# Final loads that wait for the counted blocks, a table load moved ahead of the expert blocks, and the closing additions split between two engines

## The chip, the cores and the metric

The kernel runs on one core of a Trainium2 chip. The core has five engines that run their own instruction streams and meet at semaphores: TensorE (PE) multiplies matrices into PSUM banks, VectorE (DVE) and ScalarE (ACT) read and write PSUM and SBUF, GpSimd (POOL) works on SBUF alone and issues the indirect transfers, SyncE (SP) issues most other transfers. The metric is the device time of one execution in microseconds (us); lower is better.

## The reference

A gated block on x (8 batches of 128 tokens, width 128): cross attention with 16 heads, then a mixture of 8 experts, of which each token takes 2, beside a shared expert.

```python
x = x + tanh(g_xattn) * attention(layernorm(x), ctx, ctx, mask)
n = layernorm(x)
shared = (silu(n @ shared_gate.T) * (n @ shared_up.T)) @ shared_down.T
probs = sigmoid(n @ router_w.T + routing_bias)
scores, indices = top_k(probs, 2);  scores /= scores.sum(-1)
w = zeros(tokens, 8);  w[token, indices] += scores
combined = sum over e of w[:, e] * ((silu(n @ gate_w[e]) * (n @ up_w[e])) @ down_w[e])
x = x + tanh(g_ffn) * (shared + combined)
```

The inputs are drawn from a fixed seed. Counted from the reference on them, the eight experts get 393, 406, 155, 274, 99, 207, 206 and 308 of the 2,048 choices.

## The kernel before

Everything is ordered by hand: each engine's stream is written out, with waits on named semaphores.

**Attention** takes the first 115 us or so. While its last groups run, the tokens are **routed**: batches are taken in five parts (`ROUTED`, the last, `LAST`, is batch 7). For each part PE transposes the normalised rows (`x2_transposes`) into a PSUM bank of `route_bank`, ACT copies them (`x2_split`), PE computes the router's logits, ACT takes an exponential (`route_exp`, whose last call is the last exponential of the program), DVE chooses the two experts (`choose_steps`), PE counts (`ranks`), DVE turns ranks into places (`place`), and POOL scatters the rows to a table `xs` in HBM (`scatter`), sorted by expert and cut into candidate tiles of 128 rows. `table_steps` lists which tiles exist, for full tiles of the first six batches first (`EARLY` = 5 blocks), then for the rest.

**Blocks.** The number of tiles in use depends on the data. The program always runs `BLOCKS` = 23 of them, the most that there can be; the blocks past the last existing tile read an empty tile whose row numbers point outside the result. Each block n is gathered by SP (`gather`, 8 buffers), transposed by PE (`block_transpose`), split by ACT and DVE into a high and a low part (`block_hi`, `block_lo`), multiplied with gate and up weights (`block_gate_up`), put through SiLU on ACT (`block_silu`) and a product on DVE (`block_hidden`), transposed again, copied by DVE (`block_hidT`), multiplied with the down weights (`block_down`), scaled by ACT (`block_y`), and scattered by POOL into `ys` in HBM, which counts `y_out[n % 8]` up by 16 when it has landed. PE works on several blocks at once in a software pipeline.

**The shared expert** has four units (`shared_pass(unit, part)`, `silu(unit)`, `hidden(unit)`): two of 128 hidden columns for each half of the tokens, each of six matmuls over 512 tokens; then `down_step(half)` and `add_shared(half)`, which adds a half of the tokens into `x_sb` on DVE (`acc_done`). Unit 0 runs among the blocks, units 1 to 3 after them.

**The end.** SP waits until all y scatters have landed (`y_out`), issues four loads `load_y` of 256 KB from `ys` into `y_rows` (`in_y`), DVE adds each token's two expert results to `x_sb` in four pieces, two additions each (`first_added`, `sum_ready`), and after each piece SP or ACT stores it. `stay_warm(n)` is n matmuls on a constant tile whose results nobody reads.

## Time and profile before

| | us |
|---|---|
| median of 3 runs (lowest, highest) | 181.72 (181.02, 184.23) |
| the profiled execution, whole time | 181.07 |
| its span, from the first to the last instruction | 179.3 |
| PE busy in it | 165.0 |
| DVE, ACT, POOL busy in it | 126.9, 109.3, 108.4 |
| mean granted clock of PE, 1 being full speed | 0.993 |

The profile is one execution; its rows give times from the start of the span. The whole time is 1.8 us longer than the span. An engine's busy time says how much of the span it worked, not that the end waited for it.

### The profile page before, as it was taken

What the parts mean: (1) busy time and instruction counts of PE and PEld (TensorE: products, weight loads), DVE (VectorE), ACT (ScalarE), POOL (GpSimd) and SP (SyncE); (2) the same over time, 40 slices, a digit from 0 to 9 for tenths busy, and PEclk for the clock granted to TensorE, in tenths of its full rate; (3) what the DMA queues carried; (4) which work ended last, traced back from release to release, by engine and by line L of the source; (5) the groups of instructions that cost most, each with busy time, mean ns of one, the idle gap of its engine ahead of it and who ended that gap; (6) DMA issues with size and microseconds to landing.
All of it is one profiled execution on the core that took longest, in us unless ns stands there. A gap on an engine that the chain in (4) does not pass through costs nothing.

```text
span 179.3 us, 4668 instructions
## 1 busy us (share of the span) xinstructions
PE 165.0 (92%) x1424; PEld 140.2 (78%) x1424; DVE 126.9 (71%) x613; ACT 109.3 (61%) x402; POOL 108.4 (60%) x137
## 2 busy tenths in 40 slices
PE   7899889999999999999999999988899999998960
PEld 7777669988889998779998779876586887886840
DVE  2779988756898766798776798778746666663364
ACT  3657997468588267598367698513546666663210
POOL 3666799846796816866706868686444666666200
PEclk9999999999999999999999999999999999999997
DMA  5999994900000000101000000013132222211063
GB/s 154 262 372 375 412 410 191 385 23 4 16 0 18 0 2 4 32 19 44 1 4 0 15 21 32 15 49 91 45 89 65 63 66 78 73 53 35 12 223 117
DMA packets 11095, 17.34 MB, mean 97 GB/s; under 512 B 2075, under 2 KB 6945, under 8 KB 10944
## 3 DMA queue, kind: packets, MB, share of 16 engines
q1 hardware_dynamic: 9504, 14.59, 24.0%
q0 software_dynamic: 1280, 2.20, 3.7%
q8 instruction: 12, 0.20, 0.4%
q10 hardware_dynamic: 288, 0.26, 0.4%
q14 instruction: 11, 0.09, 0.2%
HBM read 9.99 MB, written 7.51 MB: 98 GB/s over the span
## 4 chain that ended last, share of the span: by engine, by line
PE 62%; DVE 13%; ACT 8%; DMA 6%; POOL 5%; issue 4%; SPq 1%
PE misc L397 8%; PE pt L650 7%; PE s_even L360 6%; PE o_bank L386 6%; ACT probs L716 4%; PE pt L371 4%; PE proj_q L317 3%; DMA wq_raw<-wqT 3%; PE proj_k L317 3%; DVE probs L925 3%; PE proj_k L319 2%; PE pt L641 2%; PE proj_k L318 2%; PE proj_q L319 2%; PE proj_q L318 2%
## 5 line engine op out<-in xcount | busy, mean ns | idle before, releaser
L716 ACT ACTIVATE probs<-probs,negmax 128x128 f32<-128x128 f32 x128 | 50.0, 395 | 8.5 <-DVE negmax L925 8.5
L1311 POOL TENSOR_TENSOR probs<-probs,rinv 128x512 f32<-128x512 f32 x32 | 33.1, 1046 | 24.6 <-DVE rinv L939 24.3
L1420 POOL DMA_INDIRECT ys<-probsT,xg x23 | 22.5, 979 | 17.2 <-issue 10.7
L716 ACT ACTIVATION_READ_ACCUMULATOR probs<-probs,negmax 128x1 f32 x128 | 24.4, 191 | 0.0
L925 DVE CUSTOM_DVE_ANT_0 probs<-s_even,mask 128x128 f32<-128x128 f32 x64 | 18.1, 282 | 3.8 <-issue 3.8
L1341 POOL DMA_INDIRECT xs<-xrow,slot x16 | 16.3, 1019 | 6.5 <-issue 3.9
L371 PE MATMUL pt<-ident_sb,probs 128*128 128x128 f32 x128 | 17.6, 277 | 1.6 <-POOL probs L1311 1.1
L360 PE MATMUL s_odd<-kT,qT 64*128 64x128 f32 x128 | 18.5, 285 | 0.0
L360 PE MATMUL s_even<-kT,qT 64*128 64x128 f32 x128 | 18.5, 284 | 0.0
L925 DVE CUSTOM_DVE_ANT_0 probs<-s_odd,mask 128x128 f32<-128x128 f32 x64 | 18.1, 283 | 0.0
L650 PEld LDWEIGHTS pt<-down_sb,v 128*128 128x128 f32 x92 | 12.1, 190 | 7.2 <-issue 7.1
L705 ACT COPY qT<-proj_q 128x512 f32<-128x512 f32 x12 | 7.1, 588 | 16.7 <-PE proj_q L319 16.7
L360 PEld LDWEIGHTS s_even<-kT,qT 64*128 64x128 f32 x128 | 15.4, 188 | 2.1 <-issue 1.4
L371 PEld LDWEIGHTS pt<-ident_sb,probs 128*128 128x128 f32 x128 | 14.1, 141 | 3.4 <-issue 1.8
L650 PE MATMUL pt<-down_sb,v 128*128 x92 | 15.7, 293 | 1.2 <-DVE v L1237 1.2
L386 PE MATMUL o_bank<-probsT,v 128*64 128x128 f32 x240 | 16.4, 279 | 0.0
L386 PEld LDWEIGHTS o_bank<-probsT,v 128*64 128x64 f32 x240 | 12.8, 137 | 3.4 <-issue 2.5
L360 PEld LDWEIGHTS s_odd<-kT,qT 64*128 64x128 f32 x128 | 15.4, 188 | 0.0
L397 PE MATMUL misc<-wo_sb,oT 128*128 128x128 f32 x112 | 14.3, 281 | 0.9 <-DVE oT L947 0.9
L397 PEld LDWEIGHTS misc<-wo_sb,oT 128*128 128x128 f32 x112 | 13.0, 192 | 2.0 <-DVE oT L947 1.7
L912 DVE COPY kT<-proj_k 128x512 f32<-128x512 f32 x12 | 8.3, 692 | 5.7 <-PE proj_k L319 5.6
L852 ACT ACTIVATE probsT<-pt,xg 128x128 f32<-128x128 f32 x23 | 8.4, 367 | 6.2 <-PE pt L650 4.3
(279 smaller groups left out, 455.0 us busy)
## 6 DMA issues: line engine op xcount, KB each, us to landing
xs<-pad SPq DMA_DIRECT2D x5, 858.0 KB, 5.8
xg<-xs SPq DMA_DIRECT2D x23, 66.0 KB, 1.9
down_sb<-down SPq DMA_DIRECT2D x1, 1152.0 KB, 8.9
probs<-ys SPq DMA_DIRECT2D x4, 256.0 KB, 4.0
gu_raw<-gu SPq DMA_DIRECT2D x3, 256.0 KB, 6.5
wk_raw<-wkT SPq DMA_DIRECT2D x2, 256.0 KB, 3.8
wq_raw<-wqT SPq DMA_DIRECT2D x2, 256.0 KB, 5.0
mask<-mask SPq DMA_DIRECT2D x8, 64.0 KB, 2.0
```

What stands on the lines that cost most here:

```text
L317: pe.matmul(dst, a_hi, b_hi, start=True, stop=False)
L360: mm = pe.matmul(s_bank[odd][:, j * P:(j + 1) * P], qT[rows, 4 * half + j, i * P:(i + 1) * P], kT[rows, 4 * half + j, i * P:(i + 1) * P], ...
L371: mm = pe.transpose(pt_bank[u][:, j * P:(j + 1) * P], probs[:, r, 4 * u + j, :], ident_sb[:])
L386: mm = pe.matmul(o_of.get(g, o_bank)[DK * odd:DK * (odd + 1), j * P:(j + 1) * P], v_sb[i][:, h * DK:(h + 1) * DK], probsT[:, half, 2 * j + ...
L397: mm = pe.matmul(misc[:, 0:P], oT[:, c // 4, c % 4, :], wo_sb[:, c, :], start=(c == 0), stop=(c == CHUNKS - 1))
L650: mm = pe.matmul(y_bank[:, 0:P], hidT[n % 2][:, c, :], down_sb[:, bass.ds(e * I_FFN + c * P, P)], start=(c == 0), stop=(c == 1))
L716: e = act.activation(probs[:, r, l, :], probs[:, r, l, :], ACT.Exp, bias=negmax[:, r, l:l + 1], scale=-1.0, accum_out=rowsum[:, r, l:l + 1])
L852: act.activation(y_sb[n % IN_FLIGHT][:], y_bank[:, 0:P], ACT.Copy, scale=xg[n % IN_FLIGHT][:, P + 1:P + 2]).then_inc(y_ready, 1)
L925: dve.tensor_tensor_reduce(probs[:, r, l, :], s_bank[l % 2][:, (l // 2) * P:(l // 2 + 1) * P], mask_sb[r // 2][:], -1.0, HUGE, ALU.add, AL ...
L1311: pool.tensor_tensor(quad, quad, rinv[:, r, 4 * u:4 * u + 4].unsqueeze(2).to_broadcast([P, 4, P]), ALU.mult).then_inc(norm_done, 1)
L1341: pool.indirect_dma_start(out=xs, out_offset=bass.IndirectOffsetOnAxis(ap=slot[:, b, k:k + 1], axis=0), in_=xrow[:, b, k, :], in_offset=No ...
L1420: pool.indirect_dma_start(out=ys, out_offset=bass.IndirectOffsetOnAxis(ap=xg[n % IN_FLIGHT][:, P:P + 1].bitcast(U32), axis=0), in_=y_sb[n ...
```

## The change

Seven edits, all after the attention.

1. DVE computes, from the number of late tiles, how many scatters each of the eight `y_out` semaphores has counted once all **existing** blocks have landed (`quota_steps`, two small instructions after block 11's product). SP reads these eight numbers into registers and waits by them before `load_y`. It waits for all 23 scatters only at the very end, after the stores.
2. The first addition of each piece goes to POOL, directly after the loads land and with no wait for the shared expert. DVE makes the second addition of two pieces, then `add_shared` of that half, which now comes last; the stores wait for `acc_done`.
3. ACT takes a SiLU of one column (`act_scratch`) directly behind the last routing exponential. The compiler then puts SiLU's table load there instead of ahead of block 0's SiLU.
4. Shared unit 0 takes the place of `stay_warm(6)` ahead of the last routing part; unit 1 takes the place in the block loop that unit 0 had; units 2 and 3 run at the end, and both `down_step`s come after them. ACT's and DVE's parts move along: `silu(0)` and `hidden(0)` into blocks 0 and 1.
5. `ranks(LAST)` stands ahead of `block_transpose(1)`.
6. The last two routing parts use the banks `pt0` and `pt1`, which the attention leaves free, and the shared units and down steps other banks.
7. `x2_transposes` of these parts wait for those banks alone.

```diff
+FEWEST = TOKENS * TOP_K // P // IN_FLIGHT
...
-        shared_banks = [(proj_bank["q"], proj_bank["k"]), (o_bank, misc), (s_bank[0], s_bank[1]), (proj_bank["q"], proj_bank["k"])]
-        d_bank = [pt_bank[0], proj_bank["q"]]
+        shared_banks = [(proj_bank["q"], proj_bank["k"]), (proj_bank["q"], proj_bank["k"]), (o_bank, misc), (s_bank[0], s_bank[1])]
+        d_bank = [proj_bank["k"], proj_bank["q"]]
-        route_bank = [misc, misc, proj_bank["q"], proj_bank["q"], proj_bank["k"]]
+        route_bank = [misc, misc, proj_bank["q"], pt_bank[0], pt_bank[1]]
...
         def store_out(engine, n):
             tiles = slice(2 * n, 2 * n + 2)
-            engine.wait_ge(sum_ready, n + 1)
+            engine.wait_ge(acc_done, 1 + n // 2)
...
+            def quota(i):
+                return sp.value_load(quotas[0:1, i:i + 1], min_val=16 * FEWEST, max_val=16 * (FEWEST + 1))
+
+            sp.wait_ge(quota_ready, 2)
+            due = [quota(i) for i in range(IN_FLIGHT)]
             for i in range(IN_FLIGHT):
-                sp.wait_ge(y_out[i], 16 * len(range(i, BLOCKS, IN_FLIGHT)))
+                sp.wait_ge(y_out[i], due[i])
             for n in range(4):
                 load_y(sp, n)
             store_out(sp, 0)
             store_out(sp, 2)
+            for i in range(IN_FLIGHT):
+                sp.wait_ge(y_out[i], 16 * len(range(i, BLOCKS, IN_FLIGHT)))
             sp.wait_ge(out_sem, 64)
...
                 if r == LAST:
-                    pe.wait_ge(k_free, PROJ_USES * PAIRS)
+                    pe.wait_ge(pt1_free, GROUPS)
+                elif r == 3:
+                    pe.wait_ge(pt0_free, GROUPS)
                 elif r:
                     pe.wait_ge(at_ready, r)
-                if r == 3:
-                    pe.wait_ge(counts_read, 1)
...
-            stay_warm(6)
+            pe.wait_ge(counts_read, 1)
+            shared_pass(0, 0)
+            shared_pass(0, 1)
             x2_transposes(LAST)
...
             block_transpose(0)
-            block_transpose(1)
             pe.wait_ge(in_down, 16)
             pe.wait_ge(ez_ready, LAST + 1)
             ranks(LAST)
+            block_transpose(1)
             block_gate_up(0, experts[0])
             for n in range(BLOCKS):
                 if n + 2 == EARLY:
-                    pe.wait_ge(counts_read, 2)
-                    shared_pass(0, 0)
-                    shared_pass(0, 1)
+                    pe.wait_ge(h_done, 1)
+                    shared_pass(1, 0)
+                    shared_pass(1, 1)
...
             pe.wait_ge(xglo_ready, BLOCKS)
-            shared_pass(1, 0)
+            shared_pass(2, 0)
             block_down(BLOCKS - 1, experts[BLOCKS - 1])
-            shared_pass(1, 1)
-            pe.wait_ge(h_done, 1)
-            shared_pass(2, 0)
             shared_pass(2, 1)
-            down_step(0)
+            pe.wait_ge(hid_ready, BLOCKS)
             shared_pass(3, 0)
             shared_pass(3, 1)
+            down_step(0)
             down_step(1)
...
             route_exp(LAST)
+            act.activation(act_scratch[:], warm[:, 0:1], ACT.Silu)
...
+                if n == 0:
+                    silu(0)
                 if n + 2 == EARLY:
-                    silu(0)
+                    silu(1)
             block_y(BLOCKS - 1)
-            for unit in range(1, 4):
+            for unit in range(2, 4):
                 silu(unit)
...
+            def quota_steps():
+
+                beyond = float(IN_FLIGHT * FEWEST - EARLY) + 0.5
+                dve.tensor_scalar(more[:], iota_sb, beyond, upto[:, CANDIDATES - 1:], ALU.add, ALU.is_le).then_inc(quota_ready, 1)
+                dve.wait_ge(quota_ready, 1)
+                dve.tensor_scalar(quotas[:], more[:], 16.0, 16.0 * FEWEST, ALU.mult, ALU.add).then_inc(quota_ready, 1)
...
+                if n == 1:
+                    hidden(0)
...
                 if n + 1 == EARLY:
-                    hidden(0)
+                    hidden(1)
+                if n == 2 * EARLY:
+                    quota_steps()
             block_hidT(BLOCKS - 1)
-            for unit in range(1, 4):
+            for unit in range(2, 4):
                 hidden(unit)
-            add_shared(0)
-            y_of = y_rows.rearrange("p (b k) h -> p b k h", k=TOP_K)
-            for n in range(4):
-                tiles = slice(2 * n, 2 * n + 2)
-                if n == 2:
-                    add_shared(1)
-                dve.wait_ge(acc_done, 1 + n // 2)
-                dve.wait_ge(in_y[n], 16)
-                dve.tensor_tensor(x_sb[:, tiles, :], y_of[:, tiles, 0, :], x_sb[:, tiles, :], ALU.add).then_inc(first_added, 1)
-                dve.wait_ge(first_added, n + 1)
-                dve.tensor_tensor(x_sb[:, tiles, :], y_of[:, tiles, 1, :], x_sb[:, tiles, :], ALU.add).then_inc(sum_ready, 1)
+            for half in range(2):
+                for n in (2 * half, 2 * half + 1):
+                    tiles = slice(2 * n, 2 * n + 2)
+                    dve.wait_ge(first_added, n + 1)
+                    dve.tensor_tensor(x_sb[:, tiles, :], y_of[:, tiles, 1, :], x_sb[:, tiles, :], ALU.add).then_inc(second_added, 1)
+                dve.wait_ge(second_added, 2 * half + 2)
+                add_shared(half)
...
+            for n in range(4):
+                tiles = slice(2 * n, 2 * n + 2)
+                pool.wait_ge(in_y[n], 16)
+                pool.tensor_tensor(x_sb[:, tiles, :], y_of[:, tiles, 0, :], x_sb[:, tiles, :], ALU.add).then_inc(first_added, 1)
```

What this does to the order of instructions, at three places. The names of a row are the result and what it is made from; `kT` holds block products and SiLU results here, `qT` the shared products, `pt` the two banks pt0 and pt1, `probs` the loaded expert results.

ACT at the start of the blocks, before, from the last routing exponential (`ez`) to block 1's SiLU:

```order
L747 ACTIVATE ez<-s_odd 128x8 [waits hot_ready,lg_done]
L840 CAST xg_hi<-o_bank 128x128 [waits tx_done]
L840 CAST xg_hi<-misc 128x128 [waits tx_done]
L846 ACT_TABLE_LOAD
L846 ACTIVATE kT<-s_even 128x256 [waits bg_done]
L840 CAST xg_hi<-o_bank 128x128 [waits bg_done,tx_done]
L846 ACTIVATE kT<-s_odd 128x256 [waits bg_done]
```

The same stretch of ACT in the changed kernel:

```order
L758 ACTIVATE ez<-s_odd 128x8 [waits hot_ready,lg_done]
L846 ACT_TABLE_LOAD
L846 ACTIVATE act_scratch<-warm 128x1
L852 CAST xg_hi<-o_bank 128x128 [waits tx_done]
L852 CAST xg_hi<-misc 128x128 [waits tx_done]
L858 ACTIVATE kT<-s_even 128x256 [waits bg_done]
L852 CAST xg_hi<-o_bank 128x128 [waits bg_done,tx_done]
L858 ACTIVATE kT<-s_odd 128x256 [waits bg_done]
L831 ACTIVATE kT<-proj_q 128x512 [waits gu_done]
```

The table load moved ahead of the splits of blocks 0 and 1, with one small instruction behind it, and the shared unit's SiLU of 512 columns came in behind block 1's.

DVE at the end of the program, before, from the last two shared products:

```order
L1182 TENSOR_TENSOR qT<-kT,s_odd 128x512 [waits silu_done]
L1182 TENSOR_TENSOR qT<-kT,proj_k 128x512 [waits silu_done]
L1188 SCALAR_TENSOR_TENSOR x_sb<-pt,tanh_g,x_sb 128x512 [waits d_done]
L1271 TENSOR_TENSOR x_sb<-probs,x_sb 128x256 [waits in_y0,acc_done]
L1273 TENSOR_TENSOR x_sb<-probs,x_sb 128x256 [waits first_added]
L1271 TENSOR_TENSOR x_sb<-probs,x_sb 128x256 [waits in_y1,acc_done]
L1273 TENSOR_TENSOR x_sb<-probs,x_sb 128x256 [waits first_added]
L1188 SCALAR_TENSOR_TENSOR x_sb<-proj_q,tanh_g,x_sb 128x512 [waits d_done]
...
```

The same end of DVE in the changed kernel:

```order
L1203 TENSOR_TENSOR qT<-kT,misc 128x512 [waits silu_done]
L1203 TENSOR_TENSOR qT<-kT,s_odd 128x512 [waits silu_done]
L1292 TENSOR_TENSOR x_sb<-probs,x_sb 128x256 [waits first_added] x2
L1209 SCALAR_TENSOR_TENSOR x_sb<-proj_k,tanh_g,x_sb 128x512 [waits d_done,second_added]
L1292 TENSOR_TENSOR x_sb<-probs,x_sb 128x256 [waits first_added] x2
L1209 SCALAR_TENSOR_TENSOR x_sb<-proj_q,tanh_g,x_sb 128x512 [waits d_done,second_added]
```

Eight additions of 128x256 on DVE have become four, one shared product is gone from here, and the additions of the shared expert's halves close each half instead of opening it.

POOL at the end of the changed kernel (before, its last instruction is the last of the 23 scatters):

```order
L1441 DMA ys<-probsT,xg 2048x128 [waits y_ready] x23
L1447 TENSOR_TENSOR x_sb<-probs,x_sb 128x256 [waits in_y0]
L1447 TENSOR_TENSOR x_sb<-probs,x_sb 128x256 [waits in_y1]
L1447 TENSOR_TENSOR x_sb<-probs,x_sb 128x256 [waits in_y2]
L1447 TENSOR_TENSOR x_sb<-probs,x_sb 128x256 [waits in_y3]
```

The four additions stand behind all 23 scatters, and each waits for its own load.

## Rows read from the trace of the kernel before

**Rows 1.** Chain of waits, its end: start us, us, engine, result, line.

```profile
173.07 0.43 DVE x_sb L1271
173.87 0.43 DVE x_sb L1271
174.67 0.76 DVE x_sb L1188
176.70 0.42 DVE x_sb L1273
```

**Rows 2.** PE in order of time, after the blocks: start us, us, line, operation, idle before.

```profile
163.91 0.48 PE L317 MATMUL o_bank<-xn2T_hi,gu_hi 128*128 128x512 f32 x1
...
167.57 2.05 PE L571 MATMUL pt<-down_sb,qT 128*128 128x128 f32 x16
...
172.43 2.05 PE L571 MATMUL proj_q<-down_sb,qT 128*128 128x128 f32 x16 [1.41 <-DVE qT L1182]
```

**Rows 3.** POOL in order of time, scatters of blocks 20 and 22.

```profile
163.59 0.98 POOL L1420 DMA_INDIRECT ys<-probsT,xg  x1 [0.56 <-issue]
...
166.64 0.98 POOL L1420 DMA_INDIRECT ys<-probsT,xg  x1 [0.55 <-issue]
```

**Rows 4.** SP's waits: line, releaser, us in total, times, longest.

```profile
SPq L305 <- DMA ys<-probsT,xg: 11.6, 3, 8.6
```

**Rows 5.** DMA queue of the scatters from 165.9 to 168.85 us: packets, MB.

```profile
q0 software_dynamic: 64, 0.00, 1.6%
```

**Rows 6.** SP's loads of the results and ACT's last stores, by time.

```profile
168.91 1.75 SPq L219 DMA_DIRECT2D probs<-ys  x4
...
174.78 2.71 ACTq L224 DMA_DIRECT2D out<-x_sb  x2
```

**Rows 7.** Line L219, the loads: us from issue to landing.

```profile
DMA to landing us min/median/max: 3.6/4.0/4.2
```

**Rows 8.** Groups of POOL by form: count, busy us, mean ns, idle before.

```profile
L1286 POOL TENSOR_TENSOR ck_lo<-ctx_sb,ck_hi 128x256 fp32r<-128x256 f32 x3 | 2.2, 729 | 0.2
```

**Rows 9.** POOL, then DVE, in order of time, near 9 us.

```profile
8.83 1.30 POOL L1304 TENSOR_TENSOR wk_lo<-wk_raw,wk_hi 128x512 fp32r<-128x512 f32 x1 [1.65 <-ACT wk_hi L696]
...
6.99 0.73 DVE L901 TENSOR_TENSOR wq_lo<-wq_raw,wq_hi 128x512 fp32r<-128x512 f32 x1 [0.38 <-ACT wq_hi L696]
...
9.49 1.19 DVE L901 TENSOR_TENSOR wq_lo<-wq_raw,wq_hi 128x512 fp32r<-128x512 f32 x1 [0.69 <-ACT wq_hi L696]
```

**Rows 10.** ACT in order of time, at the start of the blocks.

```profile
122.47 0.18 ACT L747 ACTIVATE ez<-s_odd 128x8 f32<-128x8 f32 x1 [0.64 <-PE s_odd L437]
123.80 0.27 ACT L840 CAST xg_hi<-o_bank 128x128 fp32r<-128x128 f32 x1 [1.15 <-PE o_bank L625]
...
124.93 1.28 ACT L846 ACT_TABLE_LOAD   x1
126.22 0.38 ACT L846 ACTIVATE kT<-s_even 128x256 f32<-128x256 f32 x1
```

**Rows 11.** DVE in order of time, at the start of the blocks.

```profile
125.56 0.22 DVE L1053 TENSOR_TENSOR exists<-exists,early 128x64 f32<-128x64 f32 x1
125.82 0.29 DVE L1065 TENSOR_TENSOR_SCAN upto<-exists,none 128x64 f32<-128x64 f32 x1
126.64 0.42 DVE L1231 TENSOR_TENSOR kT<-kT,s_even 128x256 f32<-128x256 f32 x1 [0.53 <-ACT kT L846]
```

**Rows 12.** SP's gathers of blocks 5 and 6, line L289's landing, PE's transpose of block 5.

```profile
129.47 0.86 SPq L289 DMA_DIRECT2D xg<-xs  x2
...
DMA to landing us min/median/max: 1.8/1.9/2.2
...
132.44 0.27 PE L625 MATMUL misc<-ident_sb,xg 128*128 128x128 f32 x1
```

**Rows 13.** PE in order of time, the six `stay_warm` matmuls, in two passes each.

```profile
119.40 1.58 PE L584 MATMUL s_even<-warm 128*128 128x128 f32 x12 [0.45 <-issue]
```

**Rows 14.** Line L284, SP's loads of table entries into registers: ns min/median/max.

```profile
L284 SPq TENSOR_LOAD <-table x23: 267/273/457, 118.0 to 155.6; - x23
```

5 lines of the change are left out of this document (4 added, 1 removed).

## The prediction

> **What bounds the kernel now.** I read the chain of waits from its end first. From 173.07 us on it is DVE alone [rows 1]: additions of loaded results one behind the other, the second half's `add_shared` at 174.67, more additions, and the last ends at 177.12 (176.70 + 0.42). ACT's last store is issued at about 177.15 (174.78 + 2.71, less its own 0.34) [rows 6], and the span ends at 179.3: 2.2 us lie between the last DVE result and the end. Then PE in order of time [rows 2]: it leaves the blocks at 163.9, does shared units 1 to 3, stands idle for 1.41 us before the last down step and ends at 174.48 (172.43 + 2.05). Then the transfers that feed DVE: SP waits for y scatters, in one stretch for 8.6 us [rows 4], issues the four loads from 168.91 to 170.66 [rows 6], and they land 3.6 to 4.2 us after issue [rows 7], the first at 172.5. So three strands meet at 172.5 to 174.7: the loads, PE's shared expert, and DVE's own queue. Taking one away alone would give little; this change touches all three. The blocks before them run at PE's pace, 1.53 us each, and nothing in the edits makes that pace faster, so only their start can shift them.
>
> **Part 1, the loads' wait.** The counts in the reference give 4+4+2+3+1+2+2+3 = 21 tiles of 128, so blocks 21 and 22 are empty. The trace agrees: in the 2.95 us after 165.9, in which their scatters ran, the queue carried 64 packets of 0.00 MB [rows 5]. By the formula, semaphores 0 to 4 are due 48 and the others 32, which is what blocks 0 to 20 bring. POOL issued block 20's scatter at 163.59 and block 22's at 166.64 [rows 3]. The one long wait of 8.6 us began when the last gather was issued, at 157.1, so it ended at 165.7: the landing of block 20. The loads can go then instead of at 168.9, **3.1 us sooner** (3.05 by the two scatter issues). SP must read eight numbers first: 8 x 0.27 us [rows 14], 3.7 us by the slowest such row, from 157.1 on; that lies inside the 8.6 us and costs nothing. If that cover were gone it would cost 2 to 4 us. Eight waits by register instead of by constant: I take 0.05 us in all, between 0 and 0.3.
>
> **Part 2, PE at the end.** After 163.9 it now has four half units and block 22's down product, then both down steps. From 163.9 to the first down step before (167.57) were exactly four half units and that product, with a short wait for `h_done` in it; so the first down step again starts near 167.4. The two take 1.8 us each (2.05 less the overlap of 0.2), and silu(3) and hidden(3) are done under the first. PE's last result comes near **171.1 instead of 174.5**. The 1.4 us of unit 1 went to the block loop, where unit 0's were, and unit 0 went to where `stay_warm(6)` spent 1.58 us [rows 13]: six matmuls of 512 columns, which take about 1.4 us in the blocks' tail too. PE waits for the last rows there anyway, so this exchange is worth 0 (bounds -0.1 and +0.2).
>
> **Part 3, the additions.** Before, DVE had eight additions and two `add_shared` after its last product. Now POOL does four. DVE's price for a first and a second addition is 0.80 us a pair (173.87 - 173.07), of which the second is about 0.46, because it waits for the first; `add_shared` is 0.76 [rows 1]. POOL's 128x256 operation on two SBUF inputs takes 0.73 us [rows 8]; it also rounds, so a plain addition may take 0.6. I take 0.7.
>
> First without any interference, before a shift of the blocks: loads issued at 165.85, landing at 169.45, 170.2, 170.9 and 171.3 (the spread of rows 6 and 7). POOL, free since 167.6, ends its additions at 170.15, 170.9, 171.6 and 172.3. DVE takes the second piece's addition at 170.95, `add_shared(0)` from 171.4 to 172.15, the last two additions until 172.95, `add_shared(1)` until 173.7.
>
> But the two engines then work on SBUF operands at the same time, and the trace shows what that does. At 8.83 POOL began a subtraction of 1.30 us; DVE's subtraction with two SBUF inputs issued at 9.49 took 1.19 us, while the same operation at 6.99, with POOL idle, took 0.73 [rows 9]. It ended as if it had begun when POOL's ended. The Trainium skill says the same (SBUF — State Buffer, "SBUF: two separate sides"): VectorE with two SBUF inputs and GpSimd take an exclusive lock on a shared port pair, and the loser waits for a whole instruction; by that rule, the trace agrees.
>
> So DVE's and POOL's additions take turns. POOL ends pieces 0 and 1 at 170.15 and 170.85; DVE's addition of piece 0 comes from 170.8 to 171.2; POOL's piece 2 until 171.9; DVE's piece 1 until 172.3; POOL's piece 3 until 173.0, beside `add_shared(0)`, which reads PSUM and one SBUF tensor; DVE's last two until 173.8, `add_shared(1)` until 174.55. That is **0.8 us later** than without interference; I take 174.5.
>
> **Part 4, the start of the blocks.** SiLU's table load takes 1.28 us and the SiLU follows at once, at 126.22 [rows 10]. Before, PE had finished block 0's gate and up by about 125.6, so 0.6 us of it showed. Now the load runs from 122.65 to 123.93, then the one-column SiLU (0.18 us, like `ez`), so block 0's split starts at 124.1 instead of 123.80 [rows 10]: **0.3 us later**. It pushes DVE's whole queue by 0.3: the weights, the places, the late table's scan, which ended at 126.11 [rows 11] and now ends at 126.4. Block 0's SiLU starts at 125.7, but its product on DVE stands behind the scan: 126.4 instead of 126.64. So **0.25 us is won** of the 0.6 (bounds: 0.5 if DVE's queue isn't pushed, -0.3 if the push decides elsewhere). `ranks(LAST)` sooner wins nothing, since DVE asks for it later than it was ready before. The late scatters move with DVE by 0.3: gathers of block 5 issued at 129.75, landed by 131.6, while PE wants it at 132.2 (132.44 - 0.25) [rows 12]; 0.6 us of slack. `hidden(0)` in block 1 puts 0.6 us ahead of block 2's product, which eats up the 0.25 there but lies under PE's queue. `quota_steps`: two small operations at 0.22 us [rows 11] with a wait between, 0.4 us ahead of a copy that PE waits for; between 0 and 0.4, I take 0.15. Blocks: **0.1 us sooner** in sum (bounds -0.5 and +0.5).
>
> The Trainium skill (ScalarE: Activation LUTs, "What ACT_TABLE_LOAD costs") adds a drain of 1.38 us to each switch of tables, 2.66 us in all. The row shows 1.28 us and no gap.
>
> **Sum.** DVE ends at 174.5 - 0.1 = 174.4 instead of 177.12. The last two stores now go together from two queues, for which I add 0.1 to the 2.2. Span 176.7, 2.6 us less; with the 1.8 us around it 178.5, against 181.07 in the profiled execution. That one lay 0.65 us under the median of 181.72, whose three runs spread over 3 us; I take the profiled level for both. **178.5 us, 1.4% less**, 1.8% against the median. A change within 2% is about what a measurement of this kernel can't tell from none.
>
> **Rivals.**
>
> *No turns.* The first schedule of part 3: DVE ends at 173.6, time 177.7; with a POOL addition at 0.6 us 177.4. For it: `add_shared` doesn't collide, and arrivals 0.7 us apart leave gaps. Against it: rows 9. With a start shift of 0.5 as well, 177.0.
>
> *A dearer table switch.* If a drain shows in the new place, block 0's split is 1.7 us late instead of 0.3, the scan ends at 127.8, the blocks start 1.1 us later than before instead of 0.1 sooner: 179.7. That is the skill's rule cited above; against it, the old place shows 1.28 us.
>
> *The wait isn't shortened.* If the registers name all 23 blocks, or loading waits for block 22 in another way, the first load goes at 168.85 again, 3.05 us after the forecast's, and the rest follows it: 181.5, nothing gained. Rows 5 and the counts speak against it.
>
> *POOL's additions become the end* (slower). Four of them stand in line between the first landing at 169.4 and DVE's last 1.25 us (an addition, `add_shared`) and 2.3 us of store: 169.4 + 4p + 3.55 reaches the old 179.3 from p = 1.6 us. With lost turns on both engines, each addition of DVE (0.42) and a doubled price of 1.46 between, p is 1.9 and the time 182.3. It decides if an addition on POOL takes over twice its row; no row shows that.
>
> **How the numbers follow.** Forecast 0.52 (its own range 177.6 to 179.3, of which a fifth lies under 177.9, the 2% mark from 181.5); no turns, or a better start, 0.24; dearer start 0.12; wait not shortened 0.08; POOL the end 0.04. From 176.9 to 180.6 these leave out the last two and a little at the low end. Faster by over 2%: 0.11 of the forecast plus most of the second case, 0.33. Slower by over 2%: 0.02, half of the last case. Within 2%: the rest, 0.65.
>
> **What the changed profile would show.** The loads issued near 165.8 while PE still runs shared units, not near 169; PE's last down step ending near 171, without an idle of over 1 us before it; DVE's additions stretched from 0.42 to 0.6 us and more where POOL's overlap, or all at 0.42 if there are no turns; POOL's four near 0.7 us; `add_shared(1)` ending near 174.4; the table load at 122.7 with block 0's split at 124.1; no idle of PE before block 5. I am wrong most easily in the start (DVE's queue has little air there) and in how the turns fall. A third way is a slower landing of the loads, which now share the queues with the last two scatters; those carry nothing.

## The result and the profile after

The changed kernel takes **180.5 us** in the median of 20 runs (180.01 to 181.2), the kernel before 181.25 in 20 runs (180.59 to 184.23). The ratio is **0.9953, interval 0.9935 to 0.997**: 0.5% less. The gain is clear of the noise and about a third of the forecast one: the forecast was 178.5 us, 1.4% less. The measured time lies above the forecast's own range (177.6 to 179.3) and only just inside the wide one (176.9 to 180.6), which reached so far up for the sake of the rivals. The change is within the 2% that held most of the chance. The profiled execution has a span of 178.4 us (before 179.3, forecast 176.7) and 180.42 us in all.

The four loads now go out at 167.23 instead of 168.91 [rows 6]: 1.7 us sooner, not 3.05. Here are the additions on POOL, behind the last scatters of the block loop, block 20's first (start us, us, engine, line, operation, idle before):

```profile
164.19 0.98 POOL L1441 DMA_INDIRECT ys<-probsT,xg  x1 [0.58 <-issue]
...
171.00 3.13 POOL L1447 TENSOR_TENSOR x_sb<-probs,x_sb 128x256 f32<-128x256 f32 x4 [2.78 <-DMA probs<-ys]
```

Block 20's scatter went at 164.19, against 163.59 before [rows 3], so the blocks got later where 0.1 us was to be won. And SP, waiting for it, lets the loads go only 3.04 us behind it. SP's issues and its wait:

```profile
167.23 1.76 SPq L223 DMA_DIRECT2D probs<-ys  x4
...
174.37 1.79 SPq L228 DMA_DIRECT2D out<-x_sb  x2
...
SPq L314 <- DMA ys<-probsT,xg: 5.2, 1, 5.2
```

SP's eight numbers were read between 157.3 and 161.7, in 4.4 us, twice the 2.2 us of the forecast. After them SP still waited 5.2 us for block 20, so the cover of part 1 held. The four additions on POOL take 3.13 us together, one by one 0.72, 0.72, 0.90 and 0.90, and DVE's tail is this:

```profile
171.76 0.93 DVE L1292 TENSOR_TENSOR x_sb<-probs,x_sb 128x256 f32<-128x256 f32 x1 [2.26 <-POOL x_sb L1447]
172.61 0.94 DVE L1292 TENSOR_TENSOR x_sb<-probs,x_sb 128x256 f32<-128x256 f32 x1
173.59 0.75 DVE L1209 SCALAR_TENSOR_TENSOR x_sb<-proj_k,tanh_g,x_sb 128x512 f32<-128x512 f32 x1
174.26 0.75 DVE L1292 TENSOR_TENSOR x_sb<-probs,x_sb 128x256 f32<-128x256 f32 x2
175.04 0.75 DVE L1209 SCALAR_TENSOR_TENSOR x_sb<-proj_q,tanh_g,x_sb 128x512 f32<-128x512 f32 x1
```

The same addition is written 0.93 and 0.94 us long while POOL adds beside it, and 0.42 us alone [rows 1]; POOL's last two, which run beside these, are 0.18 us longer than its first two. The turns that the forecast chose are there, and both engines pay for them. DVE has nothing to do for 2.26 us before the first. On PE there is no wait any more before the last `down_step`; it ends at 171.72, against 174.48 before [rows 2]. PE, the `down_step`s and the block loop's transposes of some blocks in the middle of the loop:

```profile
145.18 0.27 PE L638 MATMUL misc<-ident_sb,xg 128*128 128x128 f32 x1
146.42 0.71 PE L663 MATMUL pt<-down_sb,v 128*128 x4 [0.28 <-DVE v L1258]
147.19 0.27 PE L638 MATMUL o_bank<-ident_sb,xg 128*128 128x128 f32 x1
...
151.80 0.27 PE L638 MATMUL misc<-ident_sb,xg 128*128 128x128 f32 x1
153.61 0.33 PE L638 MATMUL o_bank<-ident_sb,xg 128*128 128x128 f32 x1
155.32 0.27 PE L638 MATMUL misc<-ident_sb,xg 128*128 128x128 f32 x1
...
167.98 1.95 PE L582 MATMUL proj_k<-down_sb,qT 128*128 128x128 f32 x16
169.77 1.95 PE L582 MATMUL proj_q<-down_sb,qT 128*128 128x128 f32 x16
```

One transpose stands for one block. Their distance is 1.53 us; from 145.18 to 147.19 it is 2.01, and in between PE waited for `v`, DVE's copy for a down product. What held that copy up stands on DVE:

```profile
145.07 0.42 DVE L1252 TENSOR_TENSOR kT<-kT,s_odd 128x256 f32<-128x256 f32 x1 [0.53 <-ACT kT L858]
145.41 0.33 DVE L1100 TENSOR_SCALAR more<-rows_sb,upto 128x8 f32<-128x8 f32 x1
145.78 0.17 DVE L1102 TENSOR_SCALAR quotas<-more 128x8 int32<-128x8 f32 x1
145.86 0.42 DVE L1258 COPY v<-pt 128x256 f32<-128x256 f32 x1
```

`quota_steps` delays the copy by 0.45 us (0.34 us lie between product and copy in the block before), and all of it reaches PE. Around 152 there is a stall of another kind: two distances of 1.81 and 1.71, against 1.69 and 1.58 in the kernel before. Here the gather of block 18 reuses block 10's buffer and so waits for the landing of block 10's scatter. That scatter started at 148.31 and landed 3.27 us later, where most take 2.1 to 2.3; the gather was issued 0.1 us behind it, and block 18's transpose came at 153.61. What makes a landing late is the subject of the two tries at the end of the experiments. Last, ACT at the start of the blocks, which answers to rows 10:

```profile
122.71 0.18 ACT L758 ACTIVATE ez<-s_odd 128x8 f32<-128x8 f32 x1 [0.64 <-PE s_odd L448]
122.90 1.28 ACT L846 ACT_TABLE_LOAD   x1
124.20 0.20 ACT L846 ACTIVATE act_scratch<-warm 128x1 f32<-128x1 f32 x1
...
126.02 0.39 ACT L858 ACTIVATE kT<-s_even 128x256 f32<-128x256 f32 x1 [0.91 <-PE s_even L330]
```

The load takes 1.28 us and the next SiLU follows within 0.02 us: no dearer switch in the new place either, as part 4 had it.

**Where the 1.7 us between the forecast span and the measured one went.** Each term is the measured time less the forecast one.

| term | forecast | measured | us |
|---|---|---|---|
| last routing part (its transpose at 121.30, before 121.04) | 0 | +0.26 | +0.26 |
| start of the blocks won (to block 5's transpose) | -0.25 | -0.39 | -0.14 |
| `quota_steps` on PE's path | +0.15 | +0.45 | +0.30 |
| stall near 152 (longer than before) | 0 | +0.28 | +0.28 |
| block 20's scatter to the first load | 2.26 | 3.04 | +0.8 |
| first load to its landing | 3.6 | 3.7 to 3.8 | +0.1 |
| landing to DVE's end | 5.05 | 4.79 | -0.26 |
| DVE's end to the span's end | 2.3 | 2.6 | +0.3 |

They add up to 1.6 of the 1.7 us. The landings in this table are taken from the start of the first addition. The first term was there before unit 0: the logits of the part before it start at 118.67, in the kernel before at 118.36, and in the versions below that ran on equally fast chips anywhere from 118.37 to 119.19, with the same instructions. What lies around the span is another 0.2: 2.02 us in the mean of 20 runs, not 1.8.

### The profile page after: what moved, and what is told of

The parts are those of the page before. It is cut to its first block, busy times and chain, and to the rows that moved or that the text cites. A ratio compares the mean times of both kernels' runs of the same rounds, so it can differ in the third digit from the quotient of the medians.

```text
span 178.4 us, 4673 instructions
## 1 busy us (share of the span) xinstructions
PE 164.0 (92%) x1412; PEld 139.4 (78%) x1412; DVE 127.0 (71%) x611; ACT 109.3 (61%) x403; POOL 111.4 (62%) x141
## 4 chain that ended last, share of the span: by engine, by line
PE 50%; DVE 13%; ACT 9%; DMA 9%; POOL 9%; issue 6%; SPq 1%; POOLq 0%
PE misc L408 8%; PE s_even L371 6%; PE o_bank L397 6%; ACT probs L727 4%; PE pt L382 4%; DMA ys<-probsT,xg 3%; PE pt L663 3%; PE proj_q L328 3%; DMA wq_raw<-wqT 3%; PE proj_k L328 3%; DVE probs L939 3%; POOL ys L1441 2%; PE proj_k L330 2%; PE proj_k L329 2%; PE proj_q L330 2%
```

## The experiments

The theory after the result: the mechanism is right, and the gain is lost in small terms, of which `quota_steps` behind block 11's product and the slower landing of block 20's scatter are the largest. The rivals: the early wait itself is worth little, because something else ends last; POOL's share of the additions costs what the early loads win; the table load in its new place costs.

### All 23 scatters waited for

The changed kernel with constants in place of the eight registers, and neither `quota_steps` nor the reads.

```diff
-            sp.wait_ge(quota_ready, 2)
-            due = [quota(i) for i in range(IN_FLIGHT)]
             for i in range(IN_FLIGHT):
-                sp.wait_ge(y_out[i], due[i])
+                sp.wait_ge(y_out[i], 16 * len(range(i, BLOCKS, IN_FLIGHT)))
...
-                if n == 2 * EARLY:
-                    quota_steps()
```

> The changed kernel with the final loads waiting by constants for all 23 scatters, and without quota_steps and the eight register loads. Theory A (the chain load, addition, store sets the end): the first load goes behind the landing of block 22's scatter (167.25 + 2.3 in the changed kernel's trace, so 169.6 instead of 167.2), 2.4 us later, less the 0.45 us that PE stood waiting behind quota_steps: 2.0 us slower than the changed kernel, about 182.4 and 1.2 us slower than before. Theory B (something else, PE's shared expert or DVE's queue, sets the end): within 0.5 us of the changed kernel, about 180 to 181. In the profile A wants POOL's first addition near 173.2.

Measured: 181.86 us beside 181.18 for the kernel before, ratio 1.0044 (1.0023 to 1.0065). Against the changed kernel that is 0.9% more, 1.65 us. The loads went at 168.59, though block 20's scatter went at 163.23, 0.96 us sooner than in the changed kernel. SP's and POOL's rows:

```profile
163.23 0.98 POOL L1434 DMA_INDIRECT ys<-probsT,xg  x1 [0.59 <-issue]
...
168.59 1.76 SPq L223 DMA_DIRECT2D probs<-ys  x4
```

So with everything else changed, the counted wait is worth 1.65 us net of its own cost; and without it the other edits together make the kernel 0.4% slower than before. DVE ends at 176.69, 0.43 us sooner than in the kernel before, but the stores that go together and what lies around the span take that back and more. Its block loop keeps 1.53 to 1.58 us throughout, where `quota_steps` had cost 0.45.

### `quota_steps` early

```diff
-                if n == 2 * EARLY:
+                if n == 2:
                     quota_steps()
```

> The changed kernel with quota_steps behind block 3's product (n = 2) instead of block 11's, where PE has the shared unit's six matmuls ahead of it and DVE stands idle for 1.3 us. Theory A (quota_steps stalled PE: its transposes came 2.01 us apart there instead of 1.55): 0.4 us faster than the changed kernel, 180.1. Theory B (that stall was chance, like the later one of 0.3 us in both kernels): the same as the changed kernel, with a stall still in the profile.

Measured: 179.49 us, ratio 0.9901 (0.9871 to 0.9931), span 177.3: 0.9 us better than the changed kernel. PE, SP and POOL:

```profile
145.18 0.27 PE L638 MATMUL misc<-ident_sb,xg 128*128 128x128 f32 x1
146.74 0.27 PE L638 MATMUL o_bank<-ident_sb,xg 128*128 128x128 f32 x1
...
163.44 0.98 POOL L1441 DMA_INDIRECT ys<-probsT,xg  x1 [0.56 <-issue]
...
166.26 1.76 SPq L223 DMA_DIRECT2D probs<-ys  x4
```

The stall is gone; it and the smaller stall near 152 account for the 0.75 us by which the scatter is sooner (163.44 against 164.19), and 0.2 us more comes from the wait behind it, 2.82 instead of 3.04, because this landing is sooner (2.54 us against 2.76). The distance from scatter to load stays 0.6 us over the 2.26 that was expected.

### All additions on DVE, in the same order

```diff
                 for n in (2 * half, 2 * half + 1):
                     tiles = slice(2 * n, 2 * n + 2)
+                    dve.wait_ge(in_y[n], 16)
+                    dve.tensor_tensor(x_sb[:, tiles, :], y_of[:, tiles, 0, :], x_sb[:, tiles, :], ALU.add).then_inc(first_added, 1)
                     dve.wait_ge(first_added, n + 1)
...
-            for n in range(4):
-                tiles = slice(2 * n, 2 * n + 2)
-                pool.wait_ge(in_y[n], 16)
-                pool.tensor_tensor(x_sb[:, tiles, :], y_of[:, tiles, 0, :], x_sb[:, tiles, :], ALU.add).then_inc(first_added, 1)
```

> The changed kernel with the first additions on DVE again, in DVE's queue right ahead of the second ones; order of add_shared as in the changed kernel. Theory A (POOL's and DVE's additions took turns, so the second engine brought nothing): four pairs at 0.80 and two add_shared at 0.76 from the first landing at 171.0 give 175.7, where the changed kernel's DVE ends at 175.79: no change, within 0.3 us. Theory B (the two engines did overlap): 4 x 0.34 us and more longer, 1.0 to 1.5 us slower.

Measured: 180.29 us, ratio 0.994 (0.9909 to 0.9971), the same as the changed kernel's 0.9953. DVE:

```profile
171.62 0.42 DVE L1292 TENSOR_TENSOR x_sb<-probs,x_sb 128x256 f32<-128x256 f32 x1 [1.51 <-DMA probs<-ys]
...
175.71 0.75 DVE L1209 SCALAR_TENSOR_TENSOR x_sb<-proj_q,tanh_g,x_sb 128x512 f32<-128x512 f32 x1
```

From the first load's landing to DVE's end are 4.84 us (171.62 to 176.46), with both engines 4.79. The second engine brought nothing: its additions are 0.3 to 0.5 us longer than DVE's 0.42, and two of DVE's four grow to over double. POOL's share is neither the loss nor a gain.

### The counted wait alone, in the kernel before

```diff
+            sp.wait_ge(quota_ready, 2)
+            due = [quota(i) for i in range(IN_FLIGHT)]
             for i in range(IN_FLIGHT):
-                sp.wait_ge(y_out[i], 16 * len(range(i, BLOCKS, IN_FLIGHT)))
+                sp.wait_ge(y_out[i], due[i])
...
+                if n == 2:
+                    quota_steps()
```

> The kernel before with the counted wait alone (quota_steps behind block 3's product). Theory A (before, three strands met at the end, and PE's late last down step held DVE): the loads land 3 us sooner and nothing is won; 0 to 0.2 us. Theory B (the loads alone set the old end): up to 3 us faster. The profile of A has the loads issued near 166 and DVE's additions still starting at 173.

Measured: 181.31 us, ratio 1.0014 (0.9989 to 1.004): nothing. Yet the loads went 2.5 us sooner than before. SP, then DVE:

```profile
166.40 1.75 SPq L222 DMA_DIRECT2D probs<-ys  x4
...
172.09 0.69 DVE L1199 TENSOR_TENSOR qT<-kT,proj_k 128x512 f32<-128x512 f32 x1 [2.80 <-ACT kT L830]
...
173.48 0.42 DVE L1290 TENSOR_TENSOR x_sb<-probs,x_sb 128x256 f32<-128x256 f32 x1
```

The first addition still starts at 173.48, behind `add_shared(0)` and the last hidden product, which wait for PE's shared expert. This is the opening remark of the prediction on three strands as a measurement: the counted wait is worth 0 in the old order and 1.65 us in the new one. Here the scatter went at 163.99 and landed in 2.1 us, as before. From that scatter's start to DVE's end are 13.54 us, in the kernel before 13.53, so nothing of the earlier loads reaches the end. The scatter itself went 0.4 us later than before, for the most part through a longer stall near 152 (block 9's scatter landed 3.32 us after its start), with `quota_steps` early: so that stall doesn't come from `quota_steps`.

### The table load in its old place

On top of the early `quota_steps`:

```diff
             route_exp(LAST)
-            act.activation(act_scratch[:], warm[:, 0:1], ACT.Silu)
```

> The run with quota_steps behind block 3, without the one-column SiLU, so that the table load stands ahead of block 0's SiLU again. Theory A (the load's early place wins 0.25 to 0.4 us at the start of the blocks, since DVE's queue is pushed by 0.3): 0.2 to 0.4 us slower than that run, a ratio to before near 0.992. Theory B (nothing is won, DVE's scan decides): the same, 0.990. Theory C (a table switch costs more in its new place than in its old): faster than that run. In the profile A wants block 5's transpose 0.25 to 0.4 us later, counted from the last routing exponential.

Measured: 180.45 us, ratio 0.9948 (0.9918 to 0.9977), beside 0.9901 with the table load moved. Its last routing exponential came at 122.49 and block 5's transpose at 132.44: 9.95 us, against 9.60 (122.71 to 132.31) with the move. So moving the load wins 0.35 us at this place, a little more than the 0.25 of part 4. The medians differ by 0.85 us, with intervals that overlap. The two profiled executions differ by 0.68, and the rows account for that: 0.35 here, 0.32 from a longer stall near 152 (block 10's scatter landed 3.14 us after its start, against 3.07), 0.24 from a slower first load, less 0.22 for an earlier last routing part. The stall and the load aren't tied to the edit.

### Shared results first, POOL adding

On top of the early `quota_steps`: both `add_shared` as soon as PE has their results, additions after them, and one store for each piece.

```diff
-            engine.wait_ge(acc_done, 1 + n // 2)
+            engine.wait_ge(second_added, n + 1)
...
+            add_shared(0)
+            add_shared(1)
             for n in range(4):
                 tiles = slice(2 * n, 2 * n + 2)
                 dve.wait_ge(first_added, n + 1)
                 dve.tensor_tensor(x_sb[:, tiles, :], y_of[:, tiles, 1, :], x_sb[:, tiles, :], ALU.add).then_inc(second_added, 1)
...
                 pool.wait_ge(in_y[n], 16)
+                pool.wait_ge(acc_done, 1 + n // 2)
```

> The run with quota_steps behind block 3, with both add_shared ahead of the second additions (POOL keeps the first ones and waits for add_shared of their half), and each piece stored behind its second addition. Theory A (DVE stood idle for 1.9 to 2.3 us until POOL's first addition, with add_shared(0) ready before it; after the landing it did 1.5 us of add_shared on the path): POOL's and DVE's additions take turns for 4 x 0.72 + 3 x 0.42 and one more DVE addition, 4.3 to 4.6 us from the first landing against 4.8: 0.3 to 0.5 us faster, and up to 1.1 if fewer turns fall in the way. Theory B (POOL's additions in a row end the program, whatever DVE does): 4 x 0.78 + 0.5 = 3.6, so 1.1 us faster.

Measured: 179.74 us, ratio 0.9907 (0.9873 to 0.994): no gain over 0.9901. POOL, then DVE:

```profile
170.63 1.58 POOL L1447 TENSOR_TENSOR x_sb<-probs,x_sb 128x256 f32<-128x256 f32 x2 [2.65 <-DVE x_sb L1209]
172.41 1.63 POOL L1447 TENSOR_TENSOR x_sb<-probs,x_sb 128x256 f32<-128x256 f32 x2 [0.20 <-DVE x_sb L1209]
...
171.51 0.75 DVE L1209 SCALAR_TENSOR_TENSOR x_sb<-proj_q,tanh_g,x_sb 128x512 f32<-128x512 f32 x1 [1.04 <-PE proj_q L582]
172.18 2.47 DVE L1293 TENSOR_TENSOR x_sb<-probs,x_sb 128x256 f32<-128x256 f32 x4
```

DVE's second additions of pieces 0 and 1 stand behind `add_shared(1)`, which waits for PE, and POOL's pieces 2 and 3 do too. Even so the stretch from the first load to DVE's end is shorter, 7.33 us (167.32 to 174.65) against 8.43. The profiled execution loses it elsewhere: the last routing part comes 0.5 us later than in the kernel with early `quota_steps` alone (121.75 against 121.27), scatter to load takes 3.38 instead of 2.82, and behind the last DVE result are 3.25 us instead of 2.6, with SP held for 1.2 us at the program's exit by PE's queue, where the others show 0.2. The last store had landed by then. Of these losses the 0.56 us from scatter to load are a later landing, whose cause is shown below; the routing part varies by as much between kernels with the same instructions there; the exit stays open. The order gains in this tail, the kernel doesn't.

### Shared results first, all on DVE

The same, with `add_shared(1)` between the second piece and the third, and no addition on POOL:

```diff
+            add_shared(0)
+            for n in range(4):
+                tiles = slice(2 * n, 2 * n + 2)
+                if n == 2:
+                    add_shared(1)
+                dve.wait_ge(in_y[n], 16)
+                dve.wait_ge(acc_done, 1 + n // 2)
+                dve.tensor_tensor(x_sb[:, tiles, :], y_of[:, tiles, 0, :], x_sb[:, tiles, :], ALU.add).then_inc(first_added, 1)
+                dve.wait_ge(first_added, n + 1)
+                dve.tensor_tensor(x_sb[:, tiles, :], y_of[:, tiles, 1, :], x_sb[:, tiles, :], ALU.add).then_inc(second_added, 1)
```

> The run with quota_steps behind block 3, with add_shared(0) ahead of the loads' landing, add_shared(1) between the second and the third piece, and all eight additions on DVE, each piece stored behind its own. Theory A (with turns, a second engine brings nothing): 4 x 0.80 + 0.76 = 3.96 us from the first landing to DVE's end against 4.8, 0.8 us faster than that run; the stores are apart in time as before, which gives 0.2 to 0.3 back: 1.0 us, ratio to before near 0.985. Theory B (the landings of the last loads hold it): 0.4 us less than that.

Measured: **178.18 us, ratio 0.9832 (0.9796 to 0.9868)**, span 176.5; the best version here. The same kernel once more on another chip, where the kernel before takes 185.92 us:

> The run with add_shared first and all additions on DVE once more, unchanged, as the twin on the same chip. If its gain was real, the ratio to before comes out between 0.980 and 0.987 again; if it was chance, nearer 0.990, as the run with quota_steps behind block 3.

Measured: 183.16 us, ratio 0.9843 (0.9806 to 0.988). The gain stands. DVE in the first of the two, with ACT's stores:

```profile
169.25 0.75 DVE L1209 SCALAR_TENSOR_TENSOR x_sb<-proj_k,tanh_g,x_sb 128x512 f32<-128x512 f32 x1 [0.47 <-PE proj_k L582]
170.10 0.43 DVE L1295 TENSOR_TENSOR x_sb<-probs,x_sb 128x256 f32<-128x256 f32 x1
...
171.70 0.74 DVE L1209 SCALAR_TENSOR_TENSOR x_sb<-proj_q,tanh_g,x_sb 128x512 f32<-128x512 f32 x1
...
173.81 0.42 DVE L1297 TENSOR_TENSOR x_sb<-probs,x_sb 128x256 f32<-128x256 f32 x1
...
171.82 2.78 ACTq L228 DMA_DIRECT2D out<-x_sb  x2
```

`add_shared(0)` runs while the loads are in flight. From the first addition to DVE's end are 4.13 us (170.10 to 174.23), where POOL's first addition and DVE's end lay 4.79 apart, and the last stores go one by one; the span ends 2.27 us behind DVE, not 2.6. From the first load to the span's end that is 10.25 us, with early `quota_steps` alone 11.04, and the scatter comes at the same time in both (163.43, 163.44). So 0.8 of the 1.3 us between the two medians is in this tail, and 0.2 in what lies around the span. The order and the stores make the 0.8, the single engine doesn't: from the first load's landing to DVE's end are 4.23 us here and 4.29 with POOL adding in the same kind of order, against 4.86 with `add_shared` last.

### Two tries at the landing of block 20's scatter

The landing takes 2.1 us in the kernel before and with the wait alone, 2.54 to 2.76 in the changed kernel, with early `quota_steps` (with the table load moved or in place) and with all additions on DVE in either order, and 3.1 where all 23 scatters are waited for and where the shared results come first with POOL adding. One thing differs in the list of transfers. The changed kernel from block 20's scatter to the first load:

```profile
q0 software_dynamic: 64, 0.09, 8.7%
q8 instruction: 1, 0.02, 2.0%
```

In the kernel before, this stretch has the first row alone; its transfer of instructions (16 KB, about 1 us) comes at 161.2, the changed kernel's at 164.8. Theory: this transfer holds the landing up. Both tries shift it, by putting more instructions into PE's stream of the best version, once in its first microseconds and once ahead of the blocks:

```diff
-            for _ in range(WARM_UP):
+            for _ in range(10):
+                pe.matmul(misc[:, 0:8], warm[:], warm[:, 0:8], start=True, stop=True)
+            for _ in range(6):
                 pe.matmul(misc[:, 0:P], warm[:], warm[:], start=True, stop=True)
```

> The run with add_shared first and all additions on DVE, with PE's ten warm-up matmuls at the very start replaced by ten of 8 columns and six of 128: as much time within 0.3 us, but 24 more instructions ahead of everything on PE. In the changed kernel and its variants an instruction transfer of 16 KB and 1 us starts at 164.0 to 164.8, within 0.7 us after block 20's scatter, whose landing takes 2.6 to 2.8 us; in the kernel before it starts at 161.2 and block 20's scatter lands in 2.15. Theory A (the instruction transfer holds the scatter's landing up, and its time follows from the length of PE's stream): it starts 1.5 us or more earlier here, block 20's scatter lands in 2.1 to 2.3 us, the loads are issued 2.3 to 2.5 us after the scatter's start instead of 2.8, and the run is 0.3 to 0.5 us faster. Theory B (the landing is longer for another reason): the transfer moves and the 2.8 us stay; no change, or 0.1 to 0.3 us slower for the start.

```diff
-            stay_warm(5)
+            for _ in range(30):
+                pe.matmul(s_bank[0][:, 0:8], ones_bf[:], ones_bf[:, 0:8], start=True, stop=True)
```

> The run with add_shared first and all additions on DVE, with the five warm-up matmuls of 128 columns ahead of block 0's transpose (1.36 us, 20 instructions on PE) replaced by thirty bf16 matmuls of 8 columns (0.035 us each in the ranks' rows, 60 instructions). The start of the program stays as it is. Theory A (the instruction transfer near 164 holds block 20's scatter up): it starts 2 us or more earlier, the loads are issued 2.3 to 2.5 us after that scatter's start instead of 2.8, and the run is 0.3 to 0.5 us faster than its twin of this call. Theory B (another reason): the transfer moves, the 2.8 us stay, no change.

Measured: 185.05 us beside 185.82, ratio 0.9952 (0.9922 to 0.9981), and 185.79 us beside 185.92, ratio 0.9989 (0.9962 to 1.0015). Both ran on chips where the kernel before takes over 185 us, so only their ratios compare. The loads went 2.88 and 2.76 us behind block 20's scatters, as late as without the edits (2.82), and the times say nothing for the theory. But the landing itself is another matter. Here are block 20's scatter, SP's four wait instructions behind it (the first names block 20's semaphore) and the first load, in the first try and then in the best version unchanged on such a chip, with the transfers of its stretch from scatter to load at the end:

```profile
170.84 0.98 POOL L1446 DMA_INDIRECT ys<-probsT,xg  x1 [0.38 <-issue]
L314 SPq EVENT_SEMAPHORE  x4: 17/28/28, 173.0 to 173.2; - x4
173.72 1.29 SPq L223 DMA_DIRECT2D probs<-ys  x4
```

```profile
168.21 0.98 POOL L1444 DMA_INDIRECT ys<-probsT,xg  x1 [0.55 <-issue]
L314 SPq EVENT_SEMAPHORE  x4: 6/22/28, 170.4 to 171.0; - x4
171.03 1.36 SPq L223 DMA_DIRECT2D probs<-ys  x4
q0 software_dynamic: 64, 0.09, 10.2%
```

In the first try the first wait ends at 173.0, 2.15 us after the scatter's start: block 20 landed as soon as in the kernel before. The second try shows the same 2.15, and so does the unchanged best version, which on this chip has no transfer of instructions in that stretch: it had ended 0.1 us after the scatter's start. So the twin had no late landing to win back, and the comparison of times could not decide. The 2.8 us have another reason here: SP lets 0.4 to 0.5 us pass among its four waits or behind them, in all three of these profiles and in none from the faster chips, with nothing in the profile that it waits for. Why stays open.

The trace gives the start and the end of each transfer and of each landing. These are the 16 KB transfers that began 0.5 to 0.9 us after the start of one of the blocks' last six scatters (all times in us from that scatter's start), and below them block 20's scatters without one:

| version | block | transfer | landing |
|---|---|---|---|
| before | 18 | 0.67 to 1.68 | 2.76 |
| counted wait alone | 18 | 0.68 to 1.61 | 2.69 |
| changed | 20 | 0.65 to 1.68 | 2.76 |
| all 23 waited for | 20 | 0.74 to 1.97 | 3.06 |
| all on DVE, same order | 20 | 0.56 to 1.65 | 2.73 |
| early `quota_steps`; table load in place; best version | 20 | 0.53 to 1.46 | 2.54 |
| shared results first, POOL adding | 20 | 0.65 to 2.02 | 3.10 |
| first try | 18 | 0.68 to 1.61 | 2.69 |
| second try | 17 | 0.86 to 1.82 | 2.90 |
| before; counted wait alone | 20 | none | 2.12; 2.13 |
| first try; second try | 20 | none | 2.15, by SP's wait |
| best version again | 20 | ended at 0.08 | 2.15, by SP's wait |

In every row with a transfer the landing comes 1.08 us behind the transfer's end. One more such row, of block 19 in the best version again, can't be read, since the trace lacks most steps of its landing. A landing is made of 16 steps; in the changed kernel 15 of block 20's had come by 2.13, and the last alone came at 2.76. **The theory holds for the landing**: a transfer of instructions that begins beside a scatter holds it up, and where the two tries moved it away, the landing was back at 2.15. The longer stall near 152 has the same source: the 16 KB transfer before this one fell beside block 10's scatter in the changed kernel (1.04 to 1.98, landing 3.27, here 1.3 us behind the transfer's end). Where all 23 are waited for, block 10 landed at 2.90 and there is no stall.

Where the transfer falls follows PE's stream. In the best version on a slow chip it begins 0.85 us before block 20's scatter, with 24 more instructions on PE 3.2 us before it, with 40 more 4.6 us before it. The wait alone left it beside block 18, so it was the edits to PE's stream (4 to 7) that brought it beside block 20; which of them wasn't tried apart.

Both edits cost time of their own. In the first, ten matmuls of 8 columns took as long as ten of 128 had. PE's first rows, first the shifted kernel, then the best version:

```profile
1.05 4.43 PE L480 MATMUL misc<-warm 128*128 128x8 f32 x20 [1.05 <-DVE warm L1120]
5.34 2.91 PE L482 MATMUL misc<-warm 128*128 128x128 f32 x12
```

```profile
1.05 4.64 PE L480 MATMUL misc<-warm 128*128 128x128 f32 x20 [1.05 <-DVE warm L1118]
```

So the first projection began at 7.90 instead of 5.94. In the second, the granted clock fell to its lower level at 125.8 and stayed there until 132.7. Before that PE had done the thirty short matmuls from 123.59 on, two transposes and a few more short ones, with gaps, until 125.8; then it stood idle until 127.71. The stretch from 125 to 135 us, busy time of PE, weight loads, DVE, ACT and POOL, then the granted clock; first with the 8-column matmuls, then the best version on the same chip:

```profile
125.00:135.00 10.00, 7.75 (x37) 5.95 (x38) 5.97 (x26) 3.95 (x14) 3.57 (x5) 0.66 0.19 56
```

```profile
125.00:135.00 10.00, 9.31 (x55) 6.97 (x56) 7.44 (x31) 5.02 (x18) 4.87 (x5) 1.00 0.28 78
```

A mean of 0.66 is a stretch of 0.5 (1.2 GHz) and one of 1 (2.4 GHz). PE did 37 matmuls there instead of 55. The idle time, 1.92 us before block 0's gate and up, came about because ACT left a finished transpose lying for 2 us; why, the profile doesn't say.

## Why the prediction was right and wrong

**What bounds the kernel: right.** Taking one strand away alone gives little: the wait alone 0, the other edits without the wait 0.4% more time, all three together 0.5% less.

**Part 1, right in what happens, wrong in size.** The eight numbers are read under cover, blocks 21 and 22 are waited for later, and the first load goes before their scatters would let it. The step that failed is "The loads can go then instead of at 168.9, **3.1 us sooner**": it took the landing of block 20's scatter, 2.1 us, over from the kernel before. It measured 2.76, and from there to the first load are 0.28 us instead of 0.14, so the forecast gain is 0.8 us too large. The landing is late because the changed kernel's PE stream brings a 16 KB transfer of instructions beside this scatter, where before it fell beside block 18's, two blocks earlier. The sum had no term for it. Reading the eight numbers was mis-sized too (4.4 us, not 2.2), but under cover, so it cost nothing.

**Part 2: right in its time.** Shared unit 0 in the place of `stay_warm(6)` cost nothing: from the logits ahead of it to the transpose behind it are 2.68 us before (118.36 to 121.04) and 2.68 in the version with the table load in place (118.37 to 121.05), whose attention ended as early. The last `down_step` ended at 171.72, forecast 171.1 before the blocks' shift, with no idle time ahead of it; the 0.6 us between are the later blocks. What part 2 didn't ask is where a changed PE stream puts PE's transfers of instructions, and that is what cost part 1 most.

**Part 3: right, and slightly better than forecast.** The turns are there, 0.93 us for DVE's addition beside POOL's. The end came 4.79 us after the landing, forecast 5.05. The rival without turns is refuted by the same row (it needed 4.25). One row behind the turns was read too cleanly: at 6.99, where POOL was called idle, it was on a small cast until 7.19. What I did not ask is what the second engine was worth at all: the version on DVE alone is as fast. Nor did I ask whether `add_shared` belongs last: `add_shared(0)` fits under the loads. With that order and all additions on DVE the kernel gains 1.25 us over early `quota_steps` alone (0.9901 to 0.9832). With POOL adding, the same kind of order shortened the tail as much, and a late landing, a late routing part and the exit took it back.

**Part 4: the start right, `quota_steps` wrong.** The start of the blocks came 0.39 us sooner against 0.25, and 0.35 of it is lost again with the load in its old place. The load takes 1.28 us with no gap before or behind it, so neither the drain that the Trainium skill adds (ScalarE: Activation LUTs, "What ACT_TABLE_LOAD costs") nor the rival of a dearer switch is seen. The step that failed is "between 0 and 0.4, I take 0.15" for `quota_steps`. It cost 0.45 us, just over its upper bound. The rows were there: two operations of 0.22 us with a wait between, ahead of a copy that PE waits for, in a block loop that runs at PE's pace. Nothing covered them, so the upper end was the value to take. They could have stood at any block, since SP asks for the result only at 157; with them early 0.9 us came back, twice the stall. The other half is the smaller stall near 152 (0.30) and the sooner landing of block 20 (0.22), both of which go by where a transfer of instructions falls, not by `quota_steps` itself as far as these runs show.

**The end of the sum.** Two stores issued together landed in 1.9 to 2.1 us, before each in 1.7 to 1.8; I had added 0.1 for it, and DVE's end to the span's end measured 2.6 where 2.3 was forecast. And the 1.8 us around the span were taken as fixed; they became 2.02.

The mechanism that I forecast as likeliest is therefore the one that ran, with three terms mis-sized in the same direction: the way from block 20's scatter to the load (0.8, of it 0.64 the landing), `quota_steps` (0.3) and the end (0.5 with what lies around the span). The longer stall near 152 (0.28) is a late landing too; the later routing part (0.26) isn't tied to any edit.

## What to carry to other kernels

When a small operation is added to the queue of an engine that serves the bottleneck, ask which instruction of the bottleneck waits for the one behind it; if there is one, the operation costs its whole duration, and it belongs where there is slack, however late its result is needed. Where several strands end together, measure a change in the finish only with the others in place (the same wait was worth 0 and 1.65 us), and then put the work that is ready first ahead of the work that still has to arrive. When a kernel's end hangs on one landing, look in the list of transfers for one of instructions beside it, and look again after every edit to a stream. Splitting additions in SBUF over DVE and POOL is worth trying only after the price of one beside the other is known (here 0.93 instead of 0.42 us).

## What the runs showed of the hardware

A scatter by POOL with a 16 KB transfer of instructions beside it lands 1.08 us behind that transfer's end, 2.54 to 3.10 us after its start instead of 2.12 to 2.15, and only the last of its 16 steps is late (eleven landings in eleven profiles, above; beside the scatters of blocks 9 and 10 it is 1.07 to 1.30 us behind). Reading eight numbers from SBUF into SP's registers, bounds included, took 4.4 us, 0.55 us each, twice the 0.27 us of the load alone [rows 14]. What lies around the span is 2.00 to 2.02 us in the mean of the changed kernel, of the one with all 23 scatters waited for, of the one with early `quota_steps` and of the one with the table load in place, and 1.78 to 1.84 in all others; those four share additions on POOL together with stores that wait for `acc_done`, and which of it counts wasn't tried apart. The same kernel takes 181.2 us on some chips and 185.8 to 185.9 on others.
